# GNN layer: Q rows added by the gathering DMA in eight slots, and pair counts of two destination blocks packed in one PSUM value

## The reference, cut to what matters

```python
h = relu(layernorm(x))                                  # N = 512 nodes, D = 1024
feat = concat([h[src], h[dst]], axis=1)                 # E = 8704 edges, sorted by dst
e = relu(feat @ W_k + b_k)                              # k = hh: 256 edges, oo: 1280, ho: 7168
logit = (e @ W_a + b_a)[:, 0]
alpha = exp(logit - segment_max(logit)[dst]); alpha /= segment_sum(alpha)[dst]
z = segment_sum(alpha[:, None] * h[src], dst)           # over the edges of each dst
nf2 = concat([h, z], axis=1)
out = x + concat([relu(nf2[:128] @ W_hn + b_hn), relu(nf2[128:] @ W_on + b_on)])
```

## Time and profile before

| | us |
|---|---|
| median of 3 runs (range) | 567.56 (567.0 to 568.1) |
| the profiled execution, its own time | 567.12 |
| its span | 565.3 |
| PE busy | 481.7 (85%) |
| DVE busy | 360.5 (64%) |
| POOL busy | 271.3 (48%) |
| ACT busy | 173.3 (31%) |
| mean granted clock of TensorE, of full | 0.946 |

### The profile page before, as it was taken

How to read it: one execution, slowest core, us unless ns; L and a number is a source line. 1 busy time by engine, 2 the same in 40 slices (tenths; PEclk the granted TensorE clock), 3 DMA queues, 4 the chain that set the end, 5 groups by cost and what they waited for, 6 DMA issues and landing times.

```text
span 565.3 us, 5665 instructions
## 1 busy us (share of the span) xinstructions
PE 481.7 (85%) x2008; PEld 361.7 (64%) x2008; DVE 360.5 (64%) x516; ACT 173.3 (31%) x236; POOL 271.3 (48%) x221
## 2 busy tenths in 40 slices
PE   2799999989989899897785579786867999999397
PEld 2688888833434488676664467574745888888285
DVE  5713133249987687656675688797874567657644
ACT  3611321457764611221014023222212121443400
POOL 2020000326887867667766777776766563303000
PEclk9999999989998899989988689898989999999689
DMA  8998254762444455766587578678767943200412
GB/s 332 384 425 312 88 177 166 275 222 79 119 117 120 122 182 170 258 235 193 186 266 251 185 241 259 223 251 267 253 233 278 362 154 113 74 1 0 150 56 93
DMA packets 38196, 111.27 MB, mean 197 GB/s; under 512 B 13542, under 2 KB 13542, under 8 KB 32672
## 3 DMA queue, kind: packets, MB, share of 16 engines
q0 software_dynamic: 22576, 45.93, 26.1%
q1 hardware_dynamic: 9888, 53.03, 25.2%
q10 hardware_dynamic: 5712, 12.06, 5.9%
HBM read 123.80 MB, written 15.76 MB: 247 GB/s over the span
## 4 chain that ended last, share of the span: by engine, by line
PE 38%; POOL 25%; issue 15%; DMA 11%; DVE 9%; ACT 1%; POOLq 0%; ACTq 0%; DVEq 0%
PE bank L664 11%; PE bank L666 11%; PE bank L665 11%; POOL pairs_ho L858 9%; POOL gath L845 8%; POOL gath L852 8%; DMA gath<-q_ho,q_index 6%; DMA pairs_ho<-logit,cell 2%; DVE gath L470 2%; DVE gath L472 2%; DVE w_lo L424 2%; PE bank L714 2%; DMA gath<-q_oo,q_index 1%; PE bank L810 1%; PE bank L811 1%
## 5 line engine op out<-in xcount | busy, mean ns | idle before, releaser
L664 PE MATMUL bank<-w_hi,h_t 128*128 128x512 f32 x448 | 180.2, 402 | 30.9 <-DVE w_lo L424 28.6
L665 PE MATMUL bank<-w_lo,h_t 128*128 128x512 f32 x448 | 179.2, 400 | 0.0
L666 PE MATMUL bank<-w_hi,h_t 128*128 128x512 f32 x448 | 178.5, 398 | 0.0
L240 ACT ACTIVATE w_hi<-raw 128x1024 fp32r<-128x1024 f32 x80 | 80.5, 1054 | 276.2 <-PE bank L666 245.8
L424 DVE TENSOR_TENSOR w_lo<-raw,w_hi 128x1024 fp32r<-128x1024 f32 x80 | 95.1, 1228 | 67.5 <-ACT w_hi L240 67.5
L470 DVE TENSOR_TENSOR gath<-gath 128x1024 f32<-128x1024 f32 x66 | 80.9, 1226 | 83.4 <-DMA gath<-q_ho,q_index 58.7
L664 PEld LDWEIGHTS bank<-w_hi,h_t 128*128 128x128 f32 x448 | 86.8, 194 | 54.1 <-DVE w_lo L424 29.2
L845 POOL DMA_INDIRECT gath<-p_ho,i_src x56 | 68.3, 1220 | 89.8 <-DMA p_ho<-stage 65.5
L858 POOL DMA_INDIRECT pairs_ho<-logit,cell x56 | 76.8, 1371 | 48.3 <-DMA pairs_ho<-logit,cell 37.3
L666 PEld LDWEIGHTS bank<-w_hi,h_t 128*128 128x128 f32 x448 | 86.9, 194 | 18.5
L665 PEld LDWEIGHTS bank<-w_lo,h_t 128*128 128x128 f32 x448 | 86.5, 193 | 18.0
(11 more groups left out here) (118 smaller groups left out, 314.0 us busy)
## 6 DMA issues: line engine op xcount, KB each, us to landing
raw<-w_chunks SPq DMA_DIRECT2D x40, 1024.0 KB, 6.9
gath<-x SPq DMA_DIRECT2D x4, 512.0 KB, 5.1
h_dram<-h_sb SPq DMA_DIRECT2D x1, 2048.0 KB, 14.0
p_ho<-stage ACTq DMA_DIRECT2D x2, 1024.0 KB, 5.5
q_ho<-stage ACTq DMA_DIRECT2D x2, 1024.0 KB, 4.2
p_oo<-stage ACTq DMA_DIRECT2D x2, 1024.0 KB, 8.7
q_oo<-stage ACTq DMA_DIRECT2D x2, 1024.0 KB, 5.4
x_again<-x ACTq DMA_DIRECT2D x2, 1024.0 KB, 6.6
```

The lines of the kernel that those rows point to most:

```text
L240: nc.scalar.activation(w_hi[:, c % SPLIT, k], raw[:, c % RAW, k], ACT.Copy).then_inc(s_whi, 1)
L664: nc.tensor.matmul(to, hi, w_hi[:, slot, k], start=first, stop=False)
L665: nc.tensor.matmul(to, hi, w_lo[:, slot, k], start=False, stop=False)
L666: return nc.tensor.matmul(to, lo, w_hi[:, slot, k], start=False, stop=last)
```

## The change

Four parts. (1) Q's gather has `compute_op=ALU.add`: the DMA adds the Q rows to the P rows in the slot. The skipping of equal rows (`same`, `q_index`, `column`) is gone, and tile n takes column n. DVE's addition is gone. (2) There are eight slots; the Q DMA of tile n - 2 (`BEHIND`) is issued after the P rows of tile n and waits for its own P rows to land. (3) The one-hot is 256 wide: block b and block b + 1 of destinations share a column, with the value 1 for the even and 4096 (`PACK`) for the odd. PE makes half as many products, in two banks for each of four parts (the ho edges in two halves, oo, hh: `GROUPS`), opened and closed by their own first and last products. DVE takes the packed int32 sums apart with shifts and masks. (4) DVE's order: 10 tiles among the one-hots in place of 16, three groups to a tile in place of two, and `split_hi(9)` and `split_lo(9)` before the counts end. `TILES_OO` to `TILES_G` stay, so six tiles are left for L618.

```diff
+GROUPS = (0, T_HO // 4, T_HO // 2, T_NODE // 2, T_ALL // 2)
-TILES_COUNT = 16
+TILES_COUNT = 10
-SLOTS = 4
+SLOTS = 8
+BEHIND = 2
+PACK = 4096
...
-        gath = sb("gath", [P, 2, SLOTS, D], f32)
+        gath = sb("gath", [P, 2, SLOTS // 2, D], f32)
...
         @block.scalar
-            src_steps(0, 0, None)
-            src_steps(1, 1, None)
+            src_steps(0)
+            src_steps(1)
             evacuate_q(1, "ho")
             feature_hi(0)
             feature_hi(KT // 2)
+            split_hi(9)
+            for g in range(2, GROUPS[1]):
+                src_steps(g)
             act.wait_ge(s_qst, 32)
-            evacuate_sums(0, 0, 0)
-            evacuate_sums(1, 4, 1)
-            evacuate_sums(2, 4, 0)
-            split_hi(9)
+            evacuate_sums(0)
+            for g in range(GROUPS[1], GROUPS[4]):
+                src_steps(g)
+                if g == GROUPS[2] + 1:
+                    evacuate_sums(1)
+            evacuate_sums(2)
+            evacuate_sums(3)
...
         @block.vector
+            step(nc.vector.tensor_scalar(dst_block[:, 0], i_dst[:, :], 7, None, ALU.logical_shift_right))
+            step(nc.vector.tensor_scalar(dst_block[:, 1], dst_block[:, 0], 1, None, ALU.bitwise_and))
+            nc.vector.tensor_scalar(dst_at[:, 1], dst_block[:, 1], float(PACK - 1), 1.0, ALU.mult, ALU.add)
+            step(nc.vector.tensor_tensor(dst_at[:, 0], dst_block[:, 0], dst_block[:, 1], ALU.add))
+            step(nc.vector.tensor_scalar(dst_at[:, 0], dst_at[:, 0], -0.5 * P, None, ALU.mult))
+            nc.vector.tensor_tensor(dst_at[:, 0], dst_at[:, 0], f_dst[:, :], ALU.add)
...
             def edges(n):
-                slot, at = n % SLOTS, column(n)
-                dve.wait_ge(s_prow[slot], 16 * (n // SLOTS) + 16)
+                slot = n % SLOTS
                 dve.wait_ge(s_qrow[slot], 16 * (n // SLOTS) + 16)
-                p, q = edge_p[:, slot], edge_q[:, slot]
-                nc.vector.tensor_tensor(p, p, q, ALU.add).then_inc(s_esum, 1)
-                dve.wait_ge(s_esum, n + 1)
-                nc.vector.scalar_tensor_tensor(out=p, in0=p, scalar=0.0, in1=wa[:, :], op0=ALU.max, op1=ALU.mult,
-                                               accum_out=logit[:, at:at + 1]).then_inc(s_logit, 1)
+                nc.vector.scalar_tensor_tensor(out=edge[:, slot], in0=edge[:, slot], scalar=0.0, in1=wa[:, :],
+                                               op0=ALU.max, op1=ALU.mult, accum_out=logit[:, n:n + 1]
+                                               ).then_inc(s_logit, 1)
...
+                    i = nc.vector.tensor_scalar(row_dst[:, g % 2, j], node_row[:, 0:2 * P], dst_at[:, 0, t:t + 1],
+                                                dst_at[:, 1, t:t + 1], ALU.is_equal, ALU.mult)
...
+            def difference(to, n):
+                dve.wait_ge(s_cev, n + 1)
+                sums = step_sums[:, n % 2]
+                nc.vector.tensor_tensor(to[:, :, 1:N], sums[:, :, 1:N], sums[:, :, 0:N - 1], ALU.subtract)
+                for b in range(2):
+                    i = nc.vector.tensor_tensor(to[:, b, 0:1], sums[:, b, 0:1], sums[:, b, N - 1:N], ALU.add)
+                step(i)
...
+            def counts_ho():
+                difference(steps_a, 0)
+                difference(steps_b, 1)
+                upper(step_sums[:, 0], steps_a)
+                step(upper(step_sums[:, 1], steps_b))
+                nc.vector.tensor_tensor(step_sums[:, 0], step_sums[:, 0], step_sums[:, 1], ALU.add)
+                lower(None, steps_a)
+                step(lower(None, steps_b))
+                nc.vector.tensor_tensor(counts[:, 0, 0:NB:2], halves(steps_a), halves(steps_b), ALU.add)
+                step(double(counts[:, 0, 1:NB:2], step_sums[:, 0]))
...
             for n in range(TILES_COUNT):
-                for g in range(4 + 2 * n, min(6 + 2 * n, T_ALL // 2)):
-                    one_hot(g, g % 2, g - 1)
+                for g in range(4 + 3 * n, min(7 + 3 * n, GROUPS[4])):
+                    one_hot(g)
                 edges(n)
-            for n, kind in enumerate((0, 1, 2)):
-                difference(n + 1, kind, n % 2)
+            counts_ho()
+            dve.sem_inc(s_diff, 1)
+            counts_oo()
+            counts_hh()
...
         @block.tensor
+            def count_groups(n):
+                for g in range(GROUPS[n], GROUPS[n + 1]):
+                    pe.wait_ge(s_one, g + 1)
+                    pe.wait_ge(s_steps, g + 1)
+                    for j in range(2):
+                        for b in range(2):
+                            i = nc.tensor.matmul(bank[2 * n + b][:, :], row_dst[:, g % 2, j, b * P:(b + 1) * P],
+                                                 row_src[:, g % 2, j], start=g + j == GROUPS[n],
+                                                 stop=g + j == GROUPS[n + 1])
+                    i.then_inc(s_oused, 1)
...
         @block.gpsimd
+            def add_q_rows(n):
+                kind, slot = "ho" if n < T_HO else "oo", n % SLOTS
+                pool.wait_ge(s_prow[slot], 16 * (n // SLOTS) + 16)
+                nc.gpsimd.indirect_dma_start(edge[:, slot], None, node_tab[kind][1][:, :],
+                                             bass.IndirectOffsetOnAxis(ap=i_dst[:, n:n + 1], axis=0),
+                                             compute_op=ALU.add).then_inc(s_qrow[slot], 16)
...
-            for n in range(SLOTS):
-                q_rows(n)
+            for n in range(SLOTS - BEHIND):
+                add_q_rows(n)
...
                 pool.wait_ge(s_logit, n - SLOTS + 1)
                 if n < T_NODE:
                     p_rows(n)
-                    q_rows(n)
+                if n - BEHIND < T_NODE:
+                    add_q_rows(n - BEHIND)
                 if n > SLOTS:
                     pool.wait_ge(s_scat, 16 * (n - SLOTS))
                 scatter(n - SLOTS)
```

More of the change, by code:

```diff
@@ L120, in build @@
         f_dst = sb("f_dst", [P, T_ALL], f32)
-        q_index = sb("q_index", [P, T_NODE], i32)
+        dst_block = sb("dst_block", [P, 2, T_ALL], i32)
+        dst_at = sb("dst_at", [P, 2, T_ALL], f32)
         cell = sb("cell", [P, T_NODE], i32)
         logit = sb("logit", [P, T_NODE], f32)
-        same = sb("same", [P, T_NODE], f32)
         pair_hh = sb("pair_hh", [P, T_HH], i32)
@@ L133, in build @@
         den = sb("den", [P, 2, NB], f32)
-        edge_p, edge_q = gath[:, 0], gath[:, 1]
+        edge = gath[:, :, :, :].rearrange("p a s d -> p (a s) d")
         x_sb = gath[:, 0]
@@ L285, in _, with src_steps, evacuate_sums @@
             split_hi(8)
-            def src_steps(g, slot, used):
-                if used is not None:
-                    act.wait_ge(s_oused, used)
+            def src_steps(g):
+                if g >= 2:
+                    act.wait_ge(s_oused, g - 1)
                 for j in range(2):
-                    i = nc.scalar.activation(rows[:, slot, j, 0], node_row[:, :], ACT.Sign,
-                                             bias=step_at[:, bass.ds(2 * g + j, 1)])
+                    t = 2 * g + j
+                    i = nc.scalar.activation(row_src[:, g % 2, j], node_row[:, :], ACT.Sign, bias=step_at[:, t:t + 1])
                 i.then_inc(s_steps, 1)
[L296 to L301, removed]
+            def evacuate_sums(n):
+                act.wait_ge(s_oused, GROUPS[n + 1])
+                if n >= 2:
+                    act.wait_ge(s_diff, 1)
+                for b in range(2):
+                    i = nc.scalar.activation(step_sums[:, n % 2, b], bank[2 * n + b][:, :], ACT.Copy)
                 i.then_inc(s_cev, 1)
@@ L504, in one_hot @@
                 i.then_inc(s_one, 1)
[L506 to L511, removed]
-                sums = step_sums[:, slot]
-                nc.vector.tensor_tensor(counts[:, kind, :, 1:N], sums[:, :, 1:N], sums[:, :, 0:N - 1], ALU.subtract)
-                nc.vector.tensor_tensor(counts[:, kind, :, 0:1], sums[:, :, 0:1], sums[:, :, N - 1:N], ALU.add
-                                        ).then_inc(s_diff, 1)
+            one_hot(0)
@@ new lines, in _, with upper @@
+            one_hot(1)
+            def difference(to, n):
[5 more added lines that the diff above has]
+                step(i)
+            def upper(to, of):
+                return nc.vector.tensor_scalar(to, of, 13, None, ALU.logical_shift_right)
@@ new lines, in lower, with halves, double @@
+            def lower(to, of):
+                of = of.rearrange("p b n -> p (b n)").bitcast(i16).rearrange("p (b n h) -> p b n h", b=2, h=2)[:, :, :, 0]
+                return nc.vector.tensor_scalar(of if to is None else to, of, 2 * PACK - 1, None, ALU.bitwise_and)
+            def halves(of):
+                return of.rearrange("p b n -> p (b n)").bitcast(i16).rearrange("p (b n h) -> p b n h", b=2, h=2)[:, :, :, 0]
+            def double(to, of):
+                return nc.vector.tensor_scalar(to, of, 2.0, None, ALU.mult)
@@ new lines, in counts_oo, with counts_hh @@
```

(30 more changed lines are left out.)

88 lines of the change are left out of this document (28 added, 60 removed).

## The result

The changed kernel takes 607.75 us (median of 4 runs, 603.6 to 612.6) beside 567.83 for the kernel before: ratio 1.073, 95% interval 1.064 to 1.083. I had said 563, between 530 and 602. The time is just above the range, on the wrong side of no change.

A forecast was written before the change was run, and what follows sets the result against it. Three things in a row were taken as bounds: counts (PE), tile supply (POOL and the DMA array), then G (PE). Against 567.1 us, tile 52 earlier (-21) and a longer tail (+17) gave -4: 563 us, range 530 to 602.

The forecast's parts named there:

- tile 17 to tile 52: Tile supply behind the counts: next tile at 189, then 35 tiles taking 223 us of DMA work.
- tile 52 (first chunk of G waits): Start of G: tile 52 due at 412, against 433 for tile 58 before, 21 us earlier.
- the tail, longer by: After G's end: six tiles now run behind the weighing, with serial scatters and a later table load; 17 us more.
- Tiles 10 to 17 are ready when DVE returns at about 185: End of the counts: POOL fills its eight slots while DVE converts, so tile 17 is ready at 185.
- my own price: DMA array in the tile loop: with two passes for Q, a tile costs 3.8 to 5.1 us.
- Two passes for an added row: Q's gather: adding costs the array two passes of its bytes, one for each operand; main case, chance 0.5.
- The floor of the counts by ACT: Counts stage: ACT's Sign rows come last, so the counts end and OO begins at about 165, not 194.
- The cover of the conversions: Behind the counts: chunks 8 and 9, split before, keep PE busy 22 us during DVE's 19; cost at most 3.
- issuing an accumulating gather: POOL's issue of Q's gather: bounds 1.005 and 2.06 us, the lower taken since the row count is the same.
- the array at its low rate: Rival in the tile supply: two passes at 308 GB/s, tile 52 at 450, 601 us; chance 0.2.
- One pass only: Rival in the tile supply: an added row costs one pass, tile 52 at some 381, 532 us; chance 0.3.
- The 29 us of the counts: Counts stage: with half the count matmuls, OO begins at about 165 in place of 194, 29 us earlier.

The follow-up runs named there:

- the plain copy: Changed kernel with Q's gather as a plain copy that overwrites the P rows instead of adding to them: 561.1 us, ratio 0.989.
- a_skip_plain: Changed kernel with Q rows skipped where the edge before has the same destination, the others copied without accumulation: 552.3 us, ratio 0.977.
- a_skip: Changed kernel, still accumulating, with Q rows skipped where the edge before has the same destination: 560.5 us, ratio 0.992.
- c_accum: Kernel before with the accumulating gather and eight slots alone, counts and tile lists as before: 630.1 us, ratio 1.114.

## Why the prediction was wrong, by its own steps

The profiled execution took 608.3. The steps, predicted and measured:

```
                                   predicted   measured    error
tile 17 ready                          185       217.3     +32
tile 17 to tile 52                     227       232.5      +6
tile 52 (first chunk of G waits)       412       449.8     +38
tile 52 to G's end                    91.4        98.8      +7
the tail, longer by                     17        17.1       0
```

38 + 7 = 45, and 563 + 45 = 608. (91.4 is before's way from tile 58, 433.1, to G's end.)

**The step that failed** is "Tiles 10 to 17 are ready when DVE returns at about 185". Two things are wrong in it. First, it contradicts my own price. I made a tile cost the array 3.8 to 5.1 us and charged this only from 189 on; during the counts I let the stock come free. The array was at 0.92 from 119 to 150 and at 0.82 to 200, and the stock behind the tiles in work was late: the Q rows of tile 15 were issued at 186.5, where the plain copy issued them at 173.1, and landed 16 us later. (The tiles in work did not suffer: 0 to 9 came at 131.9 to 171.6, 4.4 us each, and 4.3 with the plain copy.) Second, eight slots do not mean a stock of eight. Tile n - 2 gets its Q rows only in the step of POOL's loop that waits for the logit of tile n - 8, so without new logits the Q rows of six tiles are issued, 10 to 15, and no more. The plain copy, whose array is not full, shows that rule undisguised (timeline of POOL; in brackets the idle time before):

```profile
173.12 0.99 POOL L875 DMA_INDIRECT gath<-q_ho,i_dst  x1 [0.30 <-issue]
174.73 1.33 POOL L880 DMA_INDIRECT pairs_ho<-logit,cell  x1 [0.62 <-DMA pairs_ho<-logit,cell]
187.31 1.70 POOL L867 DMA_INDIRECT gath<-p_ho,i_src  x1 [11.25 <-DVE gath L466]
```

In the changed kernel not even those six were there. Its DVE came back at 189.5, took tiles 10 to 14 without a wait and stood at tile 15 (timelines of POOL and of DVE):

```profile
186.51 2.40 POOL L875 DMA_INDIRECT gath<-q_ho,i_dst  x1 [0.30 <-issue]
...
188.86 0.69 DVE L525 TENSOR_SCALAR counts<-count_buf 128x1024 int16<-128x1024 int32 x1
189.47 1.22 DVE L466 SCALAR_TENSOR_TENSOR gath<-gath,wa 128x1024 f32<-128x1024 f32 x1
...
202.39 1.23 DVE L466 SCALAR_TENSOR_TENSOR gath<-gath,wa 128x1024 f32<-128x1024 f32 x1 [4.84 <-DMA gath<-q_ho,i_dst]
```

The runs, one trace each, share out the 32 us. With most Q rows skipped and none added (a_skip_plain) tile 17 comes at 202.7, with all of them copied at 207.6, with all of them added at 217.3. So 18 of the 32 us need neither the bytes nor the second pass: the ring and POOL's three issues a tile, which the step left out, remain for them. The bytes add 5, and the second pass with its longer issue 10.

**What was right.** Two passes for an added row, as chosen. The pace behind the counts, 6.6 us a tile where the forecast had 6.4 (223 us for 35 tiles; the 227 of the table has the 4 us from 185 to 189 in it): the array's work per tile was 65.9% of 233 us for 35 tiles, 4.4 us, between the bounds of 3.8 and 5.1, and other traffic 71 us, the lower figure that I gave. The floor of the counts by ACT: 173 in place of 165, 8 us late; groups of one-hots stood behind tile 0, for whose Q rows DVE waited 6.3 us. The chain that ended last does pass there, through ACT's signs and DVE's conversions to tile 10 at 189.5, but POOL stood idle for its logit only 0.3 us (11.25 in the plain copy, where POOL is early), so in the changed kernel little was lost by it. The cover of the conversions: from 172.8 to 189.5 DVE needed 17 us against 19, and PE ran on without a gap until 217. The tail, 17.1 us against 17: six scatters 2.9 to 4.2 apart, the load, `g_lo(3)`, and L672 at +21.5 (predicted +21).

**What was missing.** I took 1.0 us for issuing an accumulating gather, the lower bound of 1.0 and 2.06. It is 1.57, which cost 8 us where the array is free (a_skip against a_skip_plain). And G was not 86 us of PE: tiles 54 to 59 were late as well, PE waited 7.6 us for `w_lo` behind 448. I had let supply end as a bound with the start of G.

**Of the rivals**, "the array at its low rate" gave 601 and comes nearest. Its mechanism was not the one that happened: the rate was in the middle of the bounds, and 32 of the 45 missing us had been spent before 217. Its criterion, more than 227 us for the 35 tiles, was met by 6 us. "One pass only" is excluded by the packets. Even with one pass the kernel came to 561, not to the 532 that I gave, mostly because the stock was overrated there as well: tile 17 at 207.6, not 185, and tile 52 at 410, not 381.

**Where the expected gain went.** The 29 us of the counts (21 in fact) bought nothing while tiles came last: with six tiles moved the old counts gave 540.8 us and the packed ones 536.9, with ratios of 0.953 and 0.954. The kernel before already waited for tiles, and moving six or eight of them past G's start, with no other edit, gives 25 to 33 us. The change did move six, and lost that and more to an array that each tile holds for 1.5 us longer than a copy does, for bytes that the skipping of equal rows had avoided altogether. How the 64 us of c_accum split between those extra bytes and the second pass I did not measure on those counts. On the packed ones, taking away the second pass with its longer issue gives 47 us, and taking away the bytes as well 9 more (561.1 to 552.3). That these 9 are so few says that POOL's loop is the next bound; it is argued, not shown, for in the plain copy POOL still waits 65.0 us for scatters to land, and with the rows skipped 48.7.

## What to carry to other kernels

Charge a shared resource for the whole stretch in which it is used, also where another engine is said to be the bound: a stock that is "ready by then" is a claim about the rate before. Count a ring of slots by the last transfer that can be issued without the consumer, not by its length. Where every wait leads to one supply, try first to move work behind the point that needs it: a list of tile numbers gave more here (25 to 33 us) than the packed counts on top of it (5).

## What the runs showed of the hardware

An indirect DMA that adds to SBUF holds a DMA engine for 328 ns for a row of 4 KB, and a plain one for 159 (medians). Its issue takes POOL 1.57 us for 128 rows instead of 0.94, whether the rows are then skipped or not (1.60 against 1.00 with the bounds check). The byte counts in the profile do not show the second pass: 74.50 MB in both kernels, so the share of the array must be read beside the GB/s. On a full array small transfers are late too: POOL waited 81.6 us in all for scatters of 128 words to land, at most 6.4 at a time, and 31.5 with the Q rows skipped. Skipped rows still appear as packets of a few bytes: the queue's packet count is 22,576 in all of these kernels.
